# Attention in four column tiles in fp32, with four chunks in flight, in a conditioned-residual kernel

## What is computed

```python
x = x + L0(x, cond_512)   # down (256->64) and up (64->256) with weights scaled per batch, relu, plus its input
x = x + L1(x, cond_512)   # U = (cond @ W_dec + b_dec) as (257, 30); out = x @ (U V)[:256] + (U V)[256]
x = x + L2(x, cond_512)   # modulated linear, attention over heads, modulated linear
x = x + L3(x, ids, ...)   # layer norms with gathered gains, three small networks, a 1536->256->256 network

# L2, for every batch b and token n: 16 heads of 16 features
kx = modulated_linear(x, ...).reshape(B, N, 16, 16)          # queries, keys and values at once
scores = einsum("bnhd,bnjd->bnhj", kx, kx) / sqrt(16)        # 16 x 16 for each token
A = softmax(scores, axis=-1)
out = einsum("bnhj,bnjd->bnhd", A, kx).reshape(B, N, 256)
```

## Time and profile before

| | us |
|---|---|
| median of 3 runs | 1256.02 (1255.97 to 1260.46) |
| span of the profiled execution | 1259.3 |
| TensorE busy | 1159.4 (92%) |
| weight loads busy | 873.1 (69%) |
| VectorE busy | 388.3 (31%) |
| POOL busy | 206.6 (16%) |
| ScalarE busy | 98.1 (8%) |

### The profile page before, as it was taken

How to read it: one execution, slowest core, us unless ns; L and a number is a source line. 1 busy time by engine, 2 the same in 40 slices (tenths; PEclk the granted TensorE clock), 3 DMA queues, 4 the chain that set the end, 5 groups by cost and what they waited for, 6 DMA issues and landing times.

```text
span 1259.3 us, 17376 instructions
## 1 busy us (share of the span) xinstructions
PE 1159.4 (92%) x7666; PEld 873.1 (69%) x7666; DVE 388.3 (31%) x669; ACT 98.1 (8%) x129; POOL 206.6 (16%) x162
## 2 busy tenths in 40 slices
PE   5957999999999998999999999999999999979773
PEld 4624968595859686787859586877759587948531
DVE  1354061224141512333141612342142511151252
ACT  0001010011000201011000200010000100010000
POOL 0043000121023100221022100221022101030131
PEclk7556565657576757666585757666575756585687
DMA  8417033305050414114050515023130504040100
GB/s 232 145 42 159 1 70 84 94 1 152 2 126 18 102 51 100 44 37 116 20 124 1 118 35 127 18 51 103 42 84 2 133 20 100 2 102 1 50 17 17
DMA packets 96175, 86.33 MB, mean 69 GB/s; under 512 B 73282, under 2 KB 83982, under 8 KB 95974
## 3 DMA queue, kind: packets, MB, share of 16 engines
q1 hardware_dynamic: 92390, 72.61, 23.9%
q0 software_dynamic: 3712, 12.59, 3.2%
HBM read 57.86 MB, written 27.26 MB: 68 GB/s over the span
## 4 chain that ended last, share of the span: by engine, by line
PE 87%; DVE 6%; SPq 2%; ACT 2%; issue 1%; DMA 1%; POOL 1%; POOLq 0%; DVEq 0%
PE pk L629 24%; PE pk L582 23%; PE ph L602 12%; PE pp L575 3%; PE ph L575 3%; PE ph L663 3%; PE pp L613 3%; PE pp L688 2%; PE pp L726 2%; PE pp L738 2%; PE pp L673 1%; PE pp L715 1%; PE ph L751 1%; PE pp L596 1%; DVE ep L927 1%
## 5 line engine op out<-in xcount | busy, mean ns | idle before, releaser
L629 PEld LDWEIGHTS pk<-vt,bd 128*128 128x128 bf16 x3072 | 299.6, 236 | 24.6 <-issue 24.6
L582 PEld LDWEIGHTS pk<-td,bd 128*128 128x128 bf16 x3072 | 298.2, 235 | 23.7 <-issue 23.4
L582 PE MATMUL pk<-td,bd 128*128 128x16 bf16 x3072 | 298.7, 246 | 2.3 <-DMA bd<-kx_dram 2.3
L629 PE MATMUL pk<-vt,bd 128*128 128x17 bf16 x3072 | 299.9, 247 | 0.0
L423 POOL TENSOR_SCALAR ve<-mv 128x4 f32<-128x4 f32 x24 | 7.1, 297 | 612.3 <-DVE mv L980 612.1
L994 DVE RECIPROCAL rz<-pk 128x16 f32<-128x16 f32 x32 | 8.2, 257 | 279.6 <-PE pk L629 279.6
L602 PE MATMUL ph<-xnT,w 128*128 128x512 f32 x64 | 54.6, 1006 | 1.3 <-DVE xnT L1146 1.3
L1002 DVE TENSOR_REDUCE rowmax<-pk 128x64 f32<-128x1024 f32 x8 | 9.8, 1224 | 144.4 <-PE pk L582 144.4
L456 POOL TENSOR_TENSOR demod<-demod,neghalf 128x32 f32<-128x32 f32 (+1 forms) x8 | 43.4, 5428 | 58.6 <-DVE demod L912 58.6
L575 PE MATMUL ph<-attnT,owT 128*128 128x512 f32 x64 | 46.9, 899 | 5.7 <-DVE h L986 5.7
L663 PE MATMUL ph<-w,hid 128*128 128x256 f32 x128 | 39.1, 432 | 10.8 <-DVE hid L1029 10.8
(11 more groups left out here) (188 smaller groups left out, 1075.8 us busy)
## 6 DMA issues: line engine op xcount, KB each, us to landing
kx_dram<-kp SPq DMA_DIRECT2D x16, 384.0 KB, 3.5
td<-kx_dram SPq DMA_DIRECT2D x8, 768.0 KB, 4.3
bd<-kx_dram SPq DMA_DIRECT2D x64, 96.0 KB, 3.4
vt<-kx_dram SPq DMA_DIRECT2D x64, 96.0 KB, 3.9
ex_dram<-ep SPq DMA_DIRECT2D x8, 768.0 KB, 3.2
bd<-ex_dram SPq DMA_DIRECT2D x64, 96.0 KB, 3.8
xin<-in_x SPq DMA_DIRECT2D x8, 512.0 KB, 4.8
x_dram<-x SPq DMA_DIRECT2D x8, 512.0 KB, 4.0
```

Of the source, the lines that this page charges most:

```text
L582: ins = mm(pk[:, NH * g:NH * g + NH], bd[:, :, p, g], td[:, :, q, g], start=(n == 0), stop=(n == len(TERMS) - 1))
L629: ins = mm(pk[:, o:o + HD + 1], bd[:, :, p, QG * q + g], vt[:, :, r, QG * q + g], start=(n == 0), stop=(n == len(TERMS) - 1))
```

## The change

- The attention in fp32. The output of a matmul now has 32 partitions: `strips` gives 32 matmuls for half of the tokens (h), each with 32 columns of weights (two tokens' heads, kc or et, with zeros in the middle) and the block-diagonal matrix bd as 128 moving columns. Four in a row go to the four column tiles (output partitions 32r to 32r+32) and the eight of a tile add up in one PSUM bank. `scores` and `values` are `strips` with other weights.
- ScalarE makes bd itself: 16 copies of 128x512 for the keys and 16 for the values of a chunk, each scaled with a column of ownrow, which is 1 on the partitions of one batch and 0 elsewhere (`key_blocks`, `value_blocks`). kt and vt come from DRAM with one DMA each, and `keys_turned` and `values_turned` copy them into order.
- The softmax runs on 128x512 halves (`shift`, exponential, `quotients`), with the reciprocal on VectorE before the values. The weights are transposed (`quarter_turns`, four transposes of a half), and so is the output. No bf16 parts are made.
- Four chunks in flight: `step(n, a, v, d, e)`. v has the keys and scores and the first half's values; d the second half's values, the output and its projection, x2 and its layer norm; e the whole of the rest. All eleven steps are written out, and no loop is left. On every engine the operations of the four roles are interleaved one by one in a written order.
- w_dec is loaded in four parts by k (0 to 8, 8 to 16, 16 to 23, 23 to 30), issued by ScalarE once the conditioning is there. The first factors of all batches stay in SBUF (u_all); u_dram is gone. Their product runs in four column tiles and the product with V in four row tiles.
- vec_rows joins the tables: one table product of 56 rows for each chunk takes the place of L747 and L751. The last layer norm is finished on VectorE (two passes), and POOL no longer adds x2k to yn. POOL raises all the demodulation sums to their power in setup. The clearing of bd is gone. The small networks' hidden layer is computed at the end of step 0 and in step 1.

```diff
-NP = 3
-TERMS = ((0, 0), (0, 1), (1, 0), (1, 1), (0, 2), (2, 0))
...
-        bd = sb("bd", [128, 128, NP, S], BF16)
-        bd_f32 = bd[:, :, :, :].rearrange("p a c b -> p (a c b)").bitcast(F32)
-        w_dec = bd_f32[:, 0:K1 * (D + 1)].rearrange("p (k i) -> p k i", k=K1)
+        bd = sb("bd", [128, 2, SH, 128])
+        w_dec = bd[:, :, :, :].rearrange("p h s c -> p (h s c)")[:, 0:K1 * (D + 1)].rearrange("p (k i) -> p k i", k=K1)
+        ownrow = sb("ownrow", [128, 2, CB])
+        u_all = sb("u_all", [128, 2, B * K1 + 2])
...
+        def roles(n):
+
+            return [n - i if 0 <= n - i < NC else None for i in range(4)]
+
+        STEPS = range(NC + 3)
...
+        DEC_PARTS = ((0, 8), (8, 16), (16, 23), (23, K1))
...
-                bank, ks = (pk, range(0, 16)) if i % 2 == 0 else (ph, range(16, K1))
-                pe.wait_ge(s_wdec[i // 2], 16)
+                bank, (k0, k1) = (pk, ph)[i % 2], DEC_PARTS[i]
+                pe.wait_ge(s_wdec[i], 16)
                 if i == 1:
                     pe.wait_ge(vs_par, 1)
                 if i >= 2:
-                    pe.wait_ge(vs_u, 2 * i - 2)
-                for n, k in enumerate(ks):
-                    ins = mm(bank[:, 64 * n:64 * n + 64], w_dec[:, k, 128 * (i // 2):128 * (i // 2) + 128], condT,
-                             start=True, stop=True)
+                    pe.wait_ge(vs_u, i - 1)
+                for f in range(2):
+                    for k in range(k0, k1):
+                        q = 512 * f + 64 * (k - k0)
+                        ins = mm(bank[:, q:q + 64], w_dec[:, k, 128 * f:128 * f + 128], condT, start=True, stop=True)
...
-            def scores(g0, g1, b):
-                for g in range(g0, g1):
-                    for n, (p, q) in enumerate(TERMS):
-                        ins = mm(pk[:, NH * g:NH * g + NH], bd[:, :, p, g], td[:, :, q, g],
-                                 start=(n == 0), stop=(n == len(TERMS) - 1))
-                if g1 == S:
-                    ins.then_inc(p_g, 1)
...
+            def quarter_turns(h, s):
+
+                for i in range(4):
+                    o = 512 * h + 128 * i
+                    ins = tr(pk[:, o:o + 128], osb[:, h, 128 * i:128 * i + 128], ident[:, :])
+                ins.then_inc(s, 1)
+
+            def strips(h, weights, s):
+
+                for i in range(4):
+                    for pair in range(2):
+                        for r in range(4):
+                            o = 512 * h + 128 * i
+                            ins = mm(pk[32 * r:32 * r + 32, o:o + 128], weights(h, 4 * i + r)[:, 16 * pair:16 * pair + 32],
+                                     bd[:, h, 8 * i + 2 * r + pair, :], start=(i == 0 and pair == 0),
+                                     stop=(i == 3 and pair == 1), skip_group_check=True)
+                ins.then_inc(s, 1)
+
+            def scores(h, s):
+                strips(h, lambda h, q: kc[:, 16 * h + q, :], s)
+
+            def values(h, s):
+                strips(h, lambda h, q: et[:, h, q, :], s)
...
-            def values(q, b):
-
-                if b is None:
-                    return
-                if q == 0:
-                    after(pe, d_bde, b, 128)
-                    after(pe, d_v, b, 128)
-                    after(pe, v_dif, b, 2)
-                if q >= 2:
-                    pe.wait_ge(v_av, 4 * b + q - 1)
-                for g in range(QG):
-                    o = 512 * (q % 2) + (HD + 1) * g
-                    for n, (p, r) in enumerate(TERMS):
-                        ins = mm(pk[:, o:o + HD + 1], bd[:, :, p, QG * q + g], vt[:, :, r, QG * q + g],
-                                 start=(n == 0), stop=(n == len(TERMS) - 1))
-                ins.then_inc(p_av, 1)
-
...
+            act.wait_ge(s_cond, COND)
+            for i, (k0, k1) in enumerate(DEC_PARTS):
+                act.dma_start(w_dec[:, k0:k1, :], t["w_dec"][:, k0:k1, :]).then_inc(s_wdec[i], 16)
...
+            def key_blocks(h, b0, b1, s):
+
+                for b in range(b0, b1):
+                    fn(bd[:, h, :, 16 * b:16 * b + 16].rearrange("p (q z) x -> p q z x", z=2),
+                       kc[:, 16 * h:16 * h + 16, :].rearrange("p q (z x) -> p q z x", z=3)[:, :, 0:3:2, :], ACT.Copy,
+                       scale=ownrow[:, 0, b:b + 1]).then_inc(s, 1)
...
+            def value_blocks(h, b0, b1, s):
+
+                for b in range(b0, b1):
+                    fn(bd[:, h, :, 16 * b:16 * b + 16], vc[:, SH * h:SH * h + SH, :], ACT.Copy,
+                       scale=ownrow[:, 1, b:b + 1]).then_inc(s, 1)
+
+            def weights_out(h, s):
+                fn(et[:, h, :, :].rearrange("p q (z x) -> p q z x", z=3)[:, :, 0:3:2, :],
+                   pk[:, 512 * h:512 * h + 512].rearrange("p (q z x) -> p q z x", q=16, z=2), ACT.Copy).then_inc(s, 1)
+
+            def outputs_out(h, s):
+                fn(osb[:, h, :].rearrange("p (i d b) -> p i d b", i=4, b=CB),
+                   pk[:, 512 * h:512 * h + 512].rearrange("p (i b d) -> p i d b", i=4, b=CB), ACT.Copy).then_inc(s, 1)
+
+            def outputs_back(h, s):
+                fn(av[:, :, SH * h:SH * h + SH], pk[:, 512 * h:512 * h + 512].rearrange("p (s j) -> p j s", j=NH),
+                   ACT.Copy).then_inc(s, 1)
+
...
-            def shifted_scores(b):
-
-                after(ve_, p_g, b)
-                ve_.tensor_reduce(rowmax[:, :], pk[:, :].rearrange("p (s h) -> p s h", h=NH), AX.X, ALU.max
-                                  ).then_inc(v_max, 1)
-                after(ve_, v_max, b)
-                for f in range(2):
-                    h = slice(8 * f, 8 * f + 8)
-                    tt(ex[:, h, :].rearrange("p h s -> p s h"),
-                       pk[:, :].rearrange("p (s h) -> p s h", h=NH)[:, :, h],
-                       rowmax[:, :].unsqueeze(2).to_broadcast([128, S, 8]), ALU.subtract).then_inc(v_dif, 1)
-
...
+            def shift(h, c, s_max, s_sub):
+
+                sc = pk[:, 512 * h:512 * h + 512].rearrange("p (q j) -> p q j", j=NH)
+                ve_.tensor_reduce(nm[:, h, :], sc, AX.X, ALU.max, negate=True).then_inc(s_max, 1)
+                after(ve_, s_max, c)
+                tt(es[:, h, :].rearrange("p (q j) -> p q j", j=NH), sc,
+                   nm[:, h, :].unsqueeze(2).to_broadcast([128, 32, NH]), ALU.add).then_inc(s_sub, 1)
+
+            def quotients(h, c, s_sum, s_rz, s_p):
+
+                w = es[:, h, :].rearrange("p (q j) -> p q j", j=NH)
+                ve_.reduce_sum(zs[:, h, :], w, AX.X).then_inc(s_sum, 1)
+                after(ve_, s_sum, c)
+                ve_.reciprocal(rz[:, h, :], zs[:, h, :]).then_inc(s_rz, 1)
+                after(ve_, s_rz, c)
+                tt(osb[:, h, :].rearrange("p (i j b) -> p i b j", i=4, b=CB),
+                   es[:, h, :].rearrange("p (i b j) -> p i b j", i=4, b=CB),
+                   rz[:, h, :].rearrange("p (i b) -> p i b", b=CB).unsqueeze(3).to_broadcast([128, 4, CB, NH]), ALU.mult
+                   ).then_inc(s_p, 1)
```

1050 lines of the change are left out of this document (533 added, 517 removed).

## The result

| | us |
|---|---|
| median, before (4 runs) | 1255.99 |
| median, changed (4 runs) | 576.69 (572.54 to 599.54) |
| ratio | 0.4576, interval 0.4553 to 0.46 |
| span of the profiled execution | 573.0 |

The account below looks back on a forecast made before the run. TensorE was taken as the bound before and after: 205 us to step 3, five middle steps 323, step 8 49, step 9 48 and tail 43 sum to 668, scaled to 666 us; range 590 to 790.

Parts of the forecast that it names:

- The bound and its removal: TensorE, busy 92% of the span, bounds the kernel; 768 tiny bf16 pairs, 74.8 us a chunk, go.
- The kept work: TensorE's unchanged matmuls, transposes and table products in a middle step: 39.4 us at full clock.
- The price of a group: Scores and values: 64 load-and-matmul pairs over four column tiles at 50 ns, 3.2 us a group, range 2.1 to 6.85.
- The first factor and V in tiles: First factor's 16 matmuls in four column tiles, 1.6 us; V product in four row tiles, 1.2 us.
- The clock: TensorE's granted clock in middle steps taken as 0.90, between 0.80 at the old kernel's end and 1.00 in dense work.
- The sum: A middle step on TensorE: 39.4 kept plus 18.7 new, 58.1 us; over 0.90 of the clock, 64.6 us.
- Everything else stays hidden: Middle steps: ScalarE 38.7 and VectorE 38 us stay under TensorE's 58; nothing but TensorE is charged.
- The walk: One middle step traced against its waits: everything is ready before TensorE wants it, by 1 to 11 us.
- Rival F: Slower than before: ScalarE's 32 scaled block copies cost 5.2 us or more each instead of 0.716; chance 0.01.
- The ends: Setup and first steps 205 us until step 3, step 8 49, step 9 48, tail 43.
- Rival E: Better than forecast: 33 ns a pair and full clock, 53.7 us a step, 598 us in all; chance 0.14.
- rival D: Handovers: ScalarE's or VectorE's order makes TensorE wait 8 us a step, 726 us in all; chance 0.07.

Follow-up runs that it names:

- both kernels that put them back: Changed kernel plus 192 skinny bf16 load-and-matmul pairs before the scores of chunks 2 to 7, weight columns 96 bytes apart or side by side: 662.88 and 616.80 us.
- the kernel with later tables: Changed kernel with the small tables' bf16 parts cut after kx of chunk 1 and their DMAs issued behind its keys and values: 558.62 (profiled) and 560.05 us.

## Why the prediction was right and wrong

**The bound and its removal.** Right. The pairs were 74.8 us of a step, and TensorE is still the bound after (each group twice: 6.9 us a step for four more groups). Of the 89.3 us that a step lost, 63.8 are the pairs less the new work (11.0 us, below); the other 25.5 are the rest of the step, 39.5 us where 65 stood. 7.5 of these were the old first factor, the old V product and the product with vec_rows (3.55, 1.98 and 1.98), and most of what is left goes with the clock, 1.00 for 0.66. What four chunks in flight and the written-out order bring by themselves, no run separates; the old order left TensorE idle for 2.7 us of a step, so there was little for it to win there.

**The kept work.** Right. 50.55 less the new work as measured (groups 7.62 with their tile changes, the turns L559 2.3, L733 0.47, L748 0.66) leaves 39.5; the prediction had 39.4.

**The price of a group.** This is the step that failed first. The working took the earlier trace rows as "the sum of 64 weight columns (53 ns) and 64 moving columns (107 ns)" and from it 134 ns in a tile and 33 a pair; then it took 50, pulled up by the 97 ns of the bf16 pairs. Both were wrong. The load hides in one tile, in two and in four (109 ns between records in each); 134 ns is what the first interval of a group takes, and no other. A row on record spoke against the sum: L726, 32 records of 32 weight and 64 moving columns in one tile, takes 3.55 us at a granted clock of 0.50, 111 ns a record, where the sum has 134 and the moving columns alone 107. The 97 ns were no limit on handing out instructions, but weights read 384 bytes from column to column: 31 ns with columns side by side, in the same kernel. So a row of two matmuls with one interval each was read as a pace, and a row of other operands as a floor. That the two errors went the same way is why 50 ns, taken between them, lay so far above 26. Four groups with their tile changes were put at 13.9 us and take 7.6: 6.3 of the 14 us by which a step was over-priced. The range's lower bound for a group, 2.1 us, left the measured 1.9 (1.68 from its first record to its last) outside.

**The first factor and V in tiles.** 1.6 and 1.2 forecast, 0.47 and 0.66 measured: 1.7 us a step, the same mistake.

**The clock.** Forecast 0.90, measured 1.00 over all five middle steps; 6.5 us a step. The transposes, tables of 24 rows and tiled matmuls of these steps don't bring it down. The rows of the old kernel could not show this, since none of its steps was without skinny pairs; 0.80 at its end is from a stretch that is idle for 40% of the time. That skinny pairs do bring it down, though the engine is busy, is shown by both kernels that put them back.

**The sum.** 6.3 + 1.7 + 6.5, less 0.3 for the turns, is 14.2; forecast 64.6, measured 50.55.

**Everything else stays hidden.** Right. TensorE is idle for 0.17 us of a middle step. The walk had the first scores 22 us behind the end of ys' projection; they come at 21. The value blocks end at 277.0 and are asked for at 278.5, so the thinnest place has 1.4 us; making the copies twice shows 6 us of cover over a step.

**ScalarE.** The copies are listed at 0.71 us each as forecast and start every 0.62, since successive ones overlap; 35.8 us a step and not 38.7. VectorE 37.7, forecast 38. Rival F had no ground.

**The ends.** Forecast and measured: kx(0) at 75 and 63.7, step 2 at 142 and 128.2, step 3 at 205 and 187, steps 8 and 9 49 + 48 and 46.3 + 47.2, tail 43 and 39. Together 25.7 us too long. In the first term, kx(0), the two things that were named did go: the 10.18 us operation and the trip of u through DRAM. Three more were left out of the sum. The largest is the clock: the first factor's matmuls were kept at their old time, and they ran at the half clock in the kernel before and at the full one in the changed kernel. The stretch and the last group of 28, before:

```profile
40.00:60.00 20.00, 20.00 (x81) 17.06 (x80) 8.01 (x11) 0.00 (x0) 0.00 (x0) 0.50 0.14 57
...
50.43 6.23 PE L511 MATMUL ph<-xnT,bd 128*128 128x64 f32 x28
```

and after:

```profile
33.00:50.00 17.00, 17.00 (x116) 12.60 (x114) 8.84 (x12) 0.63 (x1) 0.00 (x0) 1.00 0.28 101
...
46.19 3.34 PE L487 MATMUL ph<-xnT,bd 128*128 128x64 f32 x28
```

The first factors are done 7.2 us sooner (49.7 and 57.0), though the first of them begins 12 us later (29.0 and 16.8). Behind them the scaling of w1, 2.7 us on VectorE ahead of u, is gone as well, and from u to x with V added it is 1.1 us in place of 4.5. So the largest part is the same error as in the middle steps, a clock taken from rows of the old kernel. What keeps the clock at full there no run shows. What the prediction had as SyncE's queue behind the tables in step 2 was right in kind, and the kernel with later tables shows its price, 16 us. Steps 8 and 9 and the tail were together 7.5 us too long, and no run was made for them.

**The range.** 69.4 us of the 95 too many are five middle steps, 25.7 the ends. Rival E had the right mechanism (side by side, full clock), but its steps of 53.7 us still held 33 ns a pair and the dear first factor and V (3.15 us a step, 16 in five), and its ends were 10 us too long: 598 less 26 is the measured time. The low end of 590 had no case behind it in which all the terms were low. One slip in the rivals: 8 us a step in eight steps is 64 us, so rival D would be 730 and not 726; nothing hangs on it.
